# A mixture-of-experts sort inverted on the chip by one-hot products, with rows gathered per expert tile

## What is computed

```python
xn = _layernorm(x, axis=-1)
s = _L0_attn_ref(xn, ...)      # norm, up, causal conv, silu, scan, gate, down, + xn
# the scan, for each of 128 channels d and 64 states n:
#   h = exp(delta * A) * h + (delta * u) * B;   y = sum over n of h * C
g = _silu(_L0_ffn_ref(xn, gate, w1, w2, w3))
# the experts: top 2 of 8 by xn @ gate, softmax of the two;
#   out = sum of weight * ((silu(xn @ w1[e]) * (xn @ w3[e])) @ w2[e])
x = x + s * g
```

## Time and profile before

| | us |
|---|---|
| median of 3 runs | 1536.02 (1535.4 to 1540.58) |
| the profiled execution | 1538.84 |
| its span | 1537.0 |

### The profile page before, as it was taken

The page is one execution under the profiler, slowest core; times in us unless marked ns, Lnnn a source line. Parts: engine busy times, 40 slices in busy tenths (PEclk is TensorE's granted clock), DMA queues, the critical chain, the costliest instruction groups (busy, mean ns, idle before and its releaser), DMA issues. The chain is left out here.

```text
span 1537.0 us, 21330 instructions
## 1 busy us (share of the span) xinstructions
PE 1252.3 (81%) x5608; PEld 883.0 (57%) x5608; DVE 1284.9 (84%) x1709; ACT 721.0 (47%) x1557; POOL 1024.5 (67%) x976
## 2 busy tenths in 40 slices
PE   5747655888988999899999999889988999897820
PEld 5613111666665677667666676656766777675510
DVE  6545999889888988899888988899888988888838
ACT  1444533454444555454545545454545455455611
POOL 0233788667776677767776667767775777688852
PEclk7569655899999999999999999999999999997555
DMA  9843697445473457436444744636644574744336
GB/s 241 163 124 89 167 284 199 118 124 151 128 212 113 126 142 212 131 106 211 153 133 142 212 129 126 203 97 171 183 137 115 147 227 121 222 143 120 111 120 218
DMA packets 155842, 241.04 MB, mean 157 GB/s; under 512 B 26624, under 2 KB 68224, under 8 KB 155712
## 3 DMA queue, kind: packets, MB, share of 16 engines
q10 hardware_dynamic: 94944, 144.56, 34.3%
q1 hardware_dynamic: 53952, 76.31, 16.4%
q0 software_dynamic: 6816, 18.69, 3.2%
HBM read 195.84 MB, written 43.66 MB: 156 GB/s over the span
## 5 line engine op out<-in xcount | busy, mean ns | idle before, releaser
L394 POOL TENSOR_TENSOR arena<-arena,c_rep 128x512 f32<-128x512 f32 x498 | 593.5, 1196 | 331.3 <-DVE arena L876 316.1
L876 DVE TENSOR_TENSOR_SCAN arena<-bank,carry,arena 128x512 f32<-128x512 f32 x512 | 651.9, 1273 | 28.6 <-ACT bank L614 28.5
L1105 PE MATMUL bank<-xgT,wring 128*128 128x256 f32 x2240 | 533.3, 381 | 8.0 <-DVE xn L904 5.4
L1105 PEld LDWEIGHTS bank<-xgT,wring 128*128 128x128 f32 x2240 | 425.4, 191 | 74.2 <-DVE xn L904 5.8
L614 ACT ACTIVATE bank<-arena,a_neg 128x512 f32<-128x512 f32 x512 | 354.9, 693 | 181.9 <-DVE arena L876 93.6
L866 DVE TENSOR_TENSOR arena<-bank,b_rep 128x512 f32<-128x512 f32 x512 | 350.6, 685 | 48.3 <-PE bank L1117 31.6
L1117 PE MATMUL bank<-stack,pick 128*128 128x512 f32 x512 | 288.1, 581 | 84.6 <-DVE arena L866 64.8
L1074 PE MATMUL bank<-wring,hid 128*128 128x256 f32 x1120 | 300.5, 391 | 43.2 <-ACT o_sb L560 43.2
L551 ACT ACTIVATE th<-bank 128x256 f32<-128x256 f32 x312 | 119.6, 383 | 460.5 <-PE bank L1105 394.0
L1074 PEld LDWEIGHTS bank<-wring,hid 128*128 128x128 f32 x1120 | 206.2, 191 | 145.8 <-issue 105.8
L409 POOL TENSOR_TENSOR hid<-gt,ue 128x256 f32<-128x256 f32 x312 | 249.4, 800 | 32.7 <-DVE gt L888 30.6
(11 more groups left out here) (147 smaller groups left out, 726.9 us busy)
## 6 DMA issues: line engine op xcount, KB each, us to landing
arena<-delta_d ACTq DMA_DIRECT2D x512, 256.0 KB, 3.8
wring<-in_w_all SPq DMA_DIRECT2D x64, 384.0 KB, 4.8
x_sorted<-arena SPq DMA_DIRECT2D x2, 5031.0 KB, 37.5
xg<-x_sorted ACTq DMA_DIRECT2D x39, 256.0 KB
arena<-results SPq DMA_DIRECT2D x16, 512.0 KB, 6.9
xn<-in_x SPq DMA_DIRECT2D x4, 1024.0 KB, 9.5
parts_d<-spare SPq DMA_DIRECT2D x16, 256.0 KB
tails_d<-spare SPq DMA_DIRECT2D x16, 256.0 KB
```

Source lines behind the costliest of these rows:

```text
L394: pool.tensor_tensor(p_ring[:, s % P_RING, :], h_ring[:, s % H_RING, :], of_chunk(c_rep, c, 2), ALU.mult).then_inc(s_hc, 1)
L876: v.tensor_tensor_scan(out=h_ring[:, s % H_RING, :], data0=a_bank[s % 2][:, :], data1=b_ring[:, s % B_RING, :], initial=carry[:, q:q + 1], ...
L1105: ins = pe.matmul(bank[:, m * SLOT:(m + 1) * SLOT], wring[:, kk, (2 * m + h) * P:(2 * m + h + 1) * P], xgT[:, i % 2, h, :], start=(h == 0) ...
```

## The change

The sorted copy in HBM goes. The normalized rows are stored once, in their own order (`xn_d`, four stores by SP). The slot of each token and choice is split into a half tile (78 of 128 rows each) and a place in it. In 16 batches of four blocks of 128, VectorE makes one-hot rows of the half tile and of the place, POOL multiplies the first by the token's number and by its weight, and TensorE multiplies and accumulates over all 64 blocks in one PSUM bank: column h, partition p then holds the token and the weight of slot (h, p). Batches 0 to 7 stand before the loop, on VectorE ahead of the table of tiles, on TensorE ahead of the wait for that table; batches 8 to 15 stand two each in pairs 0 to 3, on TensorE ahead of left_right or the transposes. Batches use two buffers, so that VectorE's batch b waits for TensorE's batch b-2. In pair 6, `placed` on VectorE turns the bank into the lists `dest` and `source`.

POOL gathers the rows of each half tile from `xn_d` by an indirect DMA (two per tile, issued after the turn "rows" of the tile before), in place of ACT's loads. The 64 scatters and the padding go. All products of a state with C are on POOL. The first turn of the experts is planned for pair 16 on instead of 62, with the end of the even part unchanged; the first weights are loaded from pair 13 instead of 54, and the first rows are gathered in pair 12.

```diff
-ROW = D + 2
-PADS = SH
+BLOCKS = 2 * NT
+HALVES = TILES * SH
+BATCH = 4
+BATCHES = BLOCKS // BATCH
+EARLY = 8
...
-SCATTERS_FIRST = 6
-MOE_FIRST = 62
+MOE_FIRST = 16
+PLACED_AT = 6
...
-def state_on_vector(s):
-
-    return s % 4 == 2 and s < 2 * NT - SCATTERS_FIRST
-
-
-def states(s, on_vector):
-
-    return sum(state_on_vector(i) == on_vector for i in range(s + 1))
...
-        x_sorted = nc.dram_tensor("x_sorted", [TILES * SLOT, ROW], F32).ap()
-        results = nc.dram_tensor("results", [2 * T + PADS * P, D], F32).ap()
+        xn_d = nc.dram_tensor("xn_d", [T, D], F32).ap()
+        results = nc.dram_tensor("results", [2 * T + HALVES * P, D], F32).ap()
...
+        dest = sb("dest", [P, HALVES], U32)
+        source = sb("source", [P, HALVES], U32)
+        weight = sb("weight", [P, HALVES])
+        place = sb("place", [P, HALVES])
...
+        def columns(b):
+
+            return (xg, o_sb)[b % 2][:, :, :].rearrange("p s c -> p (s c)").rearrange("p (n c) -> p n c", c=P)
+
+        def hots(b):
+
+            home = ring[:, 22:24, :].rearrange("p a t -> p (a t)") if b % 2 == 0 else b_rep[:, T - 2 * CH:T]
+            return home[:, 0:BATCH * 2 * HALVES].rearrange("p (n a h) -> p n a h", n=BATCH, a=2)
+
+        def blocks(rep, b):
+
+            return rep[:, b // (NT // BATCH), (b * BATCH) % NT:(b * BATCH) % NT + BATCH]
+
+        def batches_at(s):
+
+            return range(EARLY + 2 * s, min(EARLY + 2 * s + 2, BATCHES))
...
-            sp.wait_ge(s_pad, 2)
-            for k in range(PADS):
-                sp.dma_start(x_sorted.rearrange("(q v p) c -> v p q c", p=P, v=PADS)[k],
-                             pad_rows[:, k, :].unsqueeze(1).broadcast_to([P, TILES * SH // PADS, ROW])).then_inc(s_pre, 16)
+            for q in range(4):
+                sp.wait_ge(s_norm1, 2 * q + 2)
+                sp.dma_start(xn_d[1024 * q:1024 * q + 1024, :].rearrange("(n p) c -> p n c", p=P),
+                             xn[:, 8 * q:8 * q + 8, :]).then_inc(s_xst, 16)
...
-                if s == MOE_FIRST - 8:
+                if s == MOE_FIRST - 3:
...
-            pool.wait_ge(s_slot, 1)
-            pool.wait_ge(s_pre, 16 * PADS)
-
-            def scatter_x(j):
-
-                k, n = j // NT, j % NT
-                if j == NT:
-                    pool.wait_ge(s_scat, 16 * NT)
-                    pool.tensor_copy(xn[:, :, D].bitcast(U32), dest_i[:, 1, :])
-                    pool.tensor_copy(xn[:, :, D + 1], prob[:, 1, :]).then_inc(s_meta, 1)
-                    pool.wait_ge(s_meta, 1)
-                pool.indirect_dma_start(x_sorted, bass.IndirectOffsetOnAxis(slot_i[:, k, n:n + 1], 0),
-                                        xn[:, n, :], None).then_inc(s_scat, 16)
+
+            def values_of_halves(b):
+
+                pool.wait_ge(s_hot, 2 * b + 1)
+                shape = [P, BATCH, HALVES]
+                goals, weights = hots(b)[:, :, 0, :], hots(b)[:, :, 1, :]
+                pool.tensor_tensor(goals, weights, blocks(goal, b).unsqueeze(2).broadcast_to(shape), ALU.mult).then_inc(s_val, 1)
+                pool.wait_ge(s_val, 2 * b + 1)
+                pool.tensor_tensor(weights, weights, blocks(prob, b).unsqueeze(2).broadcast_to(shape), ALU.mult).then_inc(s_val, 1)
+
+            def gather_rows(i):
+
+                ge(pool, s_tr, i)
+                for s in range(SH):
+                    n = SH * i + s
+                    pool.indirect_dma_start(xg[:, s, :], None, xn_d,
+                                            bass.IndirectOffsetOnAxis(source[:, n:n + 1], 0)).then_inc(s_xg, 16)
...
-                    if turn == "step":
+                    if turn == "rows" and i + 1 < TILES:
+                        gather_rows(i + 1)
+                    elif turn == "step":
...
-            for j in range(SCATTERS_FIRST):
-                scatter_x(j)
+            pool.wait_ge(s_slot, 1)
+            for b in range(EARLY):
+                values_of_halves(b)
             for s in range(PAIR_COUNT):
                 if s:
-                    if not state_on_vector(s - 1):
-                        state_by_c(s - 1)
+                    state_by_c(s - 1)
                     after_turns(BY_PAIR[s - 1])
-                if s + SCATTERS_FIRST < 2 * NT:
-                    scatter_x(s + SCATTERS_FIRST)
+                for b in batches_at(s):
+                    values_of_halves(b)
+                if s == MOE_FIRST - 4:
+                    pool.wait_ge(s_placed, 5)
+                    pool.wait_ge(s_xst, 16 * 4)
+                    gather_rows(0)
                 if s % PAIRS == BIAS_AT:
                     bias_rows(s // PAIRS)
...
-            def load_rows(i):
...
+                if i == 0:
+                    act.wait_ge(s_placed, 5)
...
+            def one_hots(b):
+
+                v.wait_ge(s_slot, 1)
+                ge(v, s_perm, b - 1)
+                v.tensor_tensor(hots(b)[:, :, 1, :], blocks(slot_hi, b).unsqueeze(2).broadcast_to([P, BATCH, HALVES]),
+                                halves[:, :].unsqueeze(1).broadcast_to([P, BATCH, HALVES]), ALU.is_equal).then_inc(s_hot, 1)
+                v.tensor_tensor(columns(b), blocks(slot_lo, b).unsqueeze(2).broadcast_to([P, BATCH, P]),
+                                iota[:, :].unsqueeze(1).broadcast_to([P, BATCH, P]), ALU.is_equal).then_inc(s_hot, 1)
+
+            def placed():
+
+                goals, weights = y_bank[:, 0:HALVES], y_bank[:, HALVES:2 * HALVES]
+                v.wait_ge(s_perm, BATCHES)
+                v.tensor_scalar(place[:, :], goals, 0.5, None, ALU.is_lt).then_inc(s_placed, 1)
+                v.tensor_copy(weight[:, :], weights)
+                v.wait_ge(s_placed, 1)
+                v.scalar_tensor_tensor(out=place[:, :], in0=halves[:, :], scalar=beyond[:, :], in1=place[:, :],
+                                       op0=ALU.add, op1=ALU.mult).then_inc(s_placed, 1)
+                v.wait_ge(s_placed, 2)
+                v.scalar_tensor_tensor(out=place[:, :], in0=goals, scalar=-1.0, in1=place[:, :],
+                                       op0=ALU.add, op1=ALU.add).then_inc(s_placed, 1)
+                v.wait_ge(s_placed, 3)
+                v.tensor_copy(dest[:, :], place[:, :]).then_inc(s_placed, 1)
+                v.wait_ge(s_placed, 4)
+                v.tensor_scalar(source[:, :], dest[:, :], T - 1, None, ALU.bitwise_and).then_inc(s_placed, 1)
+
+            for b in range(EARLY):
+                one_hots(b)
...
             for s in range(PAIR_COUNT):
                 mult(s)
-                if s > 1 and state_on_vector(s - 2):
-                    state_by_c(s - 2)
                 if s:
                     scan(s - 1)
                     gates(BY_PAIR[s - 1])
+                for b in batches_at(s):
+                    one_hots(b)
+                if s == PLACED_AT:
+                    placed()
...
+            def place_batch(b):
+
+                pe.wait_ge(s_hot, 2 * b + 2)
+                pe.wait_ge(s_val, 2 * b + 2)
+                for n in range(BATCH):
+                    ins = pe.matmul(y_bank[:, 0:2 * HALVES], columns(b)[:, n, :],
+                                    hots(b)[:, n, :, :].rearrange("p a h -> p (a h)"),
+                                    start=(b == 0 and n == 0), stop=(b == BATCHES - 1 and n == BATCH - 1))
+                ins.then_inc(s_perm, 1)
+
+            for b in range(EARLY):
+                place_batch(b)
...
-                pe.wait_ge(s_hc, states(4 * q + 3, False))
-                ge(pe, s_hcv, states(4 * q + 3, True))
+                pe.wait_ge(s_hc, 4 * q + 4)
+                if q == 0:
+                    pe.wait_ge(s_placed, 3)
                 if i == 0:
-                    pe.wait_ge(s_bcev, 2)
...
             for s in range(PAIR_COUNT):
                 if s + 1 < PAIR_COUNT:
                     spread(s + 1)
+                for b in batches_at(s):
+                    place_batch(b)
                 if s % 2 == 0 and s <= 2 * (NC - 2):
                     left_right(s // 2 + 1)
```

More of the change, by code:

```diff
@@ L165, in mamba_and_experts @@
         colsT = (xgT[:, :, :, :].rearrange("p a h t -> p a (h t)"), tails)
-        prob, slot_i, dest_i = (route[:, 2 * k:2 * k + 2, :] for k in range(3))
-        slot_i, dest_i = slot_i.bitcast(U32), dest_i.bitcast(U32)
+        prob, slot_hi, slot_lo, goal = (route[:, 2 * k:2 * k + 2, :] for k in range(4))
         ring = arena[:, :].rearrange("p (r t) -> p r t", t=CH)
@@ L557, in evict_out @@
                 act.wait_ge(s_o, KS * (i + 1))
+                if i == 0:
+                    act.wait_ge(s_placed, 5)
                 ge(act, s_res, 16 * SH * i)
                 for s in range(SH):
[L560 removed]
+                    ins = act.activation(o_sb[:, s, :], o_bank[:, s * D:(s + 1) * D], ACT.Identity,
+                                         scale=weight[:, SH * i + s:SH * i + s + 1])
                 ins.then_inc(s_oev, 1)
@@ L648, in _ @@
             v.wait_ge(s_first, 16 * 3)
-            v.wait_ge(s_pad, 1)
```

(17 more changed lines are left out.)

59 lines of the change are left out of this document (21 added, 38 removed).

## The result

The changed kernel takes 1547.5 us in the median of nine runs, the kernel before 1540.9 in nine runs beside it: ratio 1.0047, interval 1.0032 to 1.0061. So it is slower by 0.5%, 6.6 us, where 13 were forecast. Profiled spans are 1543.2 and 1537.0 us.

A forecast was written before the change was run, and what follows sets the result against it. VectorE alone was taken as the bound from 167 us, VectorE and TensorE together from 275 us. Terms +15 + 20 - 26 - 7 + 6 + 5 = +13 us on the median of 1536.0 gave 1549 us, range 1518 to 1574.

The forecast's parts named there:

- The batches, +35: One-hot batches at 3.1 us each, VectorE and POOL one after the other: +15 before the loop, +20 in pairs 0 to 3.
- the +20 of the loop: Batches 8 to 15 delay TensorE: +8 to 9 in pair 0, +8 in pair 2, +2 each in pairs 1 and 3.
- side by side: Rival, chance 0.20: POOL and VectorE overlap in the batches, +6 and +12 instead of +15 and +20; 1532 us.
- State products, -7: State products move from VectorE to POOL; 11 of 14, at 0.68 us, lie where VectorE is the bound: -7 us.
- Chunk 0's work beside POOL, +6: VectorE's split and silu parts in chunk 0 meet POOL's products once steps run beside them: +6 us, bounds 0 and 8.
- Fewer adjacent steps, -26: Expert steps spread over 468 pairs lie less often in adjacent pairs, so waits fall from 106 to 79 us: -26.
- The rival's bound of -66: Rival "the waits nearly vanish", chance 0.14: TensorE's slack also removes second steps' waits, -66 in place of -26; 1509 us.
- Gathers, 0: 78 gathers on POOL, 1.0 us each and 0.2 of issue, are hidden before the last 28 pairs: no cost.
- POOL becomes late: Rival, chance 0.13: POOL falls behind some 3.5 us a tile, 0.5 of it reaching TensorE through hid: +20, 1569 us.
- The last 28 pairs, +5: Three tiles' gathers take 7 us on a POOL with 11 us idle at the end: +5 us, bounds 0 and 10.
- ScalarE and SP, 0: ACT's two fewer issues a tile taken at 0, not over 3; SP's stores and weight loads hidden, at most 3 us late.
- the signs that were named: In the changed profile: loop start at 115 us, tanh waits near 65; wrong if start before 110, waits under 50 or over 85.

The follow-up runs named there:

- version with late experts: The changed kernel with the experts from pair 62 on again instead of 16, all else the same: 1561.2 us, 1.0147 of the kernel before.
- base version: Changed kernel with 4 batches ahead of the loop instead of 8, and TensorE's batches in it behind left_right or transposes: 1534.5 us, 0.9970.
- The last version: The base version with transfers spread, down rows added a pair earlier, step 3 never right behind step 2, POOL's hidden product before its state product: 1438.5 us, 0.9333.

## Why the prediction was right in the time, and wrong in two of its terms

The forecast of 1549 lies 1.5 us from what was measured. Some of that is luck: mis-sized terms offset each other, and the kernel before took 1540.9 us in the runs beside it, not the 1536.0 that the forecast was added to. As a change, +13 was forecast and +6.6 measured.

- *The batches, +35.* Pair 16 came 17.8 us later: +11.6 at the first scan (forecast 15), +13.2 for the eight in the loop (forecast 20), and -7.0 in pairs 0 to 15 that no term foresaw. The loop began on TensorE at 109.5 us, not at 115, and by the prediction's own words it is wrong there (it was to be wrong under 110). The step that failed is the price of a batch, 3.1 us against 2.25 ahead of the loop. That VectorE and POOL work one after the other was right. But POOL's two products cost 1.4 us and not the estimated 1.9, and with VectorE's 1.2 that makes 2.6; the rest, 0.3, is the start of each operation, which passes beside the one before it. The same price stands in the +20 of the loop. The mechanism of the loop (TensorE's batches ahead of left_right) was right: moved behind, a batch costs half. The -7.0 comes in the main from left_right, which the prediction read at 4.7 and 5.4 us; at the higher clock it takes 3.70, and after the change more of them ran there. The rival "side by side" had +18 for all this and hit the sum, by a mechanism that the lines speak against.
- *State products, -7.* Pairs 16 to 65 fell by 6.6 us in the version with late experts.
- *Chunk 0's work beside POOL, +6.* The parts of split there took 6.9 us instead of 4.8: +2. Half of such parts fall in pairs without a step, and those run unstretched.
- *Fewer adjacent steps, -26.* By the version with late experts against the kernel after, the waits fell by 22 us. The counting by place was sound; taken alone, with chunk 0's work in it, the earlier start gave -17.7 us from pair 16 on, for which the forecast's terms, -26 and +6, would give -20. (The rival's bound of -66 does not follow from the rates beside it: with the waits of second steps gone too they give -77, and that rival's time would be 1498 us, not 1509.)
- *Gathers, 0.* This failed. In the base version they cost 22 us, 16 of them in the stretch where the prediction called them hidden, for POOL's 70% is an average, and POOL answers in every pair: a tile's transfers keep it for 2.5 and 2.7 us. ScalarE's copy for the step after next waits for the hidden product behind them; that way 5.4 us of the gates' waits came up to pair 484, and 8.8 came through the tanh, by a path that no run separates. The rival "POOL becomes late", at 0.13 and +20, had the right engine and nearly the right size; it should have stood in the sum. Its argument against, that products out lag three steps, looked at TensorE and left out ScalarE's copy, which has two buffers.
- *The last 28 pairs, +5.* 4.4, and without the gathers 0.
- *ScalarE and SP, 0.* Nothing in the trace speaks against it.

By the stretches of the traces the sum closes. The batches and what goes with them gave 17.8 (forecast 35), the state products -6.6 (-7), pairs 65 to 484 in the version with late experts 9.2 (0), the last pairs there 4.0 (5), and the earlier start -17.7 (-20). Together that is 6.7 us where 13 were forecast. The batches stood 17 us too high and the gathers' stretch 9 too low. Taken off in the base version, where the experts start early, the gathers gave 16 in that stretch; why that is more than 9 is not shown.

Of the signs that were named: the gates' wait for the tanh was to be near 65 us and came to 82.8, just under the bound of 85 (with the waits for the copy it is over that); pairs 65 to 484 took 2.60 us each, not 2.55; pairs 16 to 65 2.4, not 2.6; POOL 70%, as forecast.

What stays open: in which steps the gathers' 22 us arise. Spread out, they mostly leave ScalarE's copy alone, and part of the time comes back in waits for the tanh, behind TensorE; and the reordering of POOL gained in another way. The last version was not run without gathers. Nor does any run explain the small product on VectorE that ended in the middle of POOL's.

## What to carry to other kernels

An engine that is busy 70% of the time is not free: ask for each instruction put on it how late the next small one behind it may be, and who holds only two buffers for that. Where VectorE and GpSimd both work from SBUF, order them so that the engine that bounds the kernel starts first; look for the loss in the mean duration of one form in different neighbourhoods, not among the waits. And when a bank or buffer is shared by turns, empty it as soon as it is full, for the next turn but one pays.

## What the runs showed that was not expected

- One reordering on GpSimd, with the same instructions, took 50 us out of VectorE's part of conv, silu and split: 128x512 operations on SBUF went from 1.0 to 1.7 us in the mean to about 0.7.
- Indirect gathers of 128 rows cost GpSimd 1.00 us each and 0.16 to 0.30 us of issue, but 22 us / 78 = 0.28 us each of the kernel's time, with GpSimd at 70%.
- TensorE spent 72 instead of 27 us at the lower clock in pairs 64 to 484 without a cost that the runs could show; where left_right sets the pace, in pairs 0 to 13 of the kernel before, four of seven ran in part at the lower clock and took 5.7 us more than at 3.70 each.
- The edits together, without touching the work done, bring the changed kernel to 1438.5 us, 0.9333 of the kernel before.
